# Six of the sixteen products of ones at the head become 22 rounds of eight small products

## The chip, the core and the metric

The kernel runs on one core of a Trainium2 chip. The metric is the device time of one execution in microseconds (us), the median of several runs. The core has five engines with queues of their own: TensorE (PE, with its weight loads listed apart as PEld), VectorE (DVE), ScalarE (ACT), GpSimd (POOL) and SyncE (SP), which here only issues DMAs.

## What is computed

One decoder layer in float32 on x of shape (2, 1024, 256), that is 2048 tokens in 16 tiles of 128:

```python
x = x + attn(layernorm(x), w_qkv, w_out, alpha, beta)   # two decaying prefix scans per channel
x = x + xattn(layernorm(x), ctx, ctx, fside, mask, ...) # 16 heads of 64, 154 keys
x = x + ffn(layernorm(x), ...)                          # 8 experts, top 2, and one shared expert
```

The first step projects the normed tokens to q, k, v; q and k go through elu(.)+1; k and k*v are scanned along time with a decay per head (`out[t] = d*out[t-1] + x[t]`), once with alpha and once with beta; the scans are multiplied by q, divided by their sums over a head and multiplied by w_out. The change touches none of this: the products of ones write a part of PSUM that nothing reads before it is overwritten.

## The kernel before

All work is written out by hand, one instruction list per engine, with semaphores between them. PSUM is one tensor `pb` of eight banks of 512 float32 per partition; a small helper, `Banks`, hands the banks out in turn from bank 0. `w.wait_ge(sem, n)` makes an engine wait.

The tokens of the first step go in four chunks of 512 (`c` = 0 to 3). For a chunk, VectorE takes means and variances of x (L1086, L1088), GpSimd makes the reciprocal roots (L1660 to L1665), ScalarE and VectorE write the normed rows `xn` (L841, L1098), TensorE transposes them (`turned`, L394), ScalarE copies the result to `xnT` (L831), and TensorE projects it (`project`, L440). ScalarE turns k and q into phi (L870, L871), VectorE multiplies (L1118, L1125) and scans (L1140). `densum` (L458) sums over a head with a matrix of 128 rows by 32 columns, `divided` (L469) spreads the result back with tiles of 32 rows.

TensorE's list starts with the function that the change edits, and then the first products that need data:

```python
idle_products()   # 16 products of ones, all to bank 7
keys(0, 2)        # L409: waits for ctxT and the first half of Wk
turned(1, 0)      # L394: waits for xn of chunk 0
project(0, "k", 0, 2)
scan_rest(0)
```

`idle_products` waits only for the fill of `ones` by GpSimd (L1714), so it runs while the first inputs are on their way. `keys(0, 2)` writes banks 0 and 1, `turned(1, 0)` banks 2 and 3, and the projections begin with bank 4. No semaphore ties the products of ones to what follows: TensorE's own order does.

Every float32 product stands in the trace as two records of PE and two of PEld; a transpose stands as one of each.

Later, in cross attention, `product` (L565 and L569) holds the only place where products on tiles of 32 rows and 64 columns are issued. In each call eight products of 128 rows by 64 columns are followed by eight of 32 rows by 64 columns, each of these on another tile of the array, with 256 columns streamed.

Of the kernel before, what the change touches and what calls it, by code (L numbers as in the profile page):

```python
# [171 lines left out]
def decoder(nc, A, xs, out):  # L172
    with ExitStack() as ctx:
        def sb(name, shape, dt=F32):
            return ctx.enter_context(nc.sbuf_tensor(name, shape, dt))
# [7 lines left out]
        pb = ctx.enter_context(nc.psum_tensor("pb", [P, 8, 512], F32))  # L183
# [6 lines left out]
        ones = sb("ones", [P, P])  # L190
# [190 lines left out]
        def _(e):  # L381
# [271 lines left out]

            def idle_products():
                w.wait_ge(zeroed.sem, zeroed["ones"])
                for _ in range(16):
                    e.matmul(pb[:, 7, 0:P], ones[:, :], ones[:, :], start=True, stop=True)

            idle_products()
            keys(0, 2)  # L660
            turned(1, 0)
# [1345 lines left out]
```

## Time and profile before

| what | value |
|---|---|
| median of three runs | 582.8 us (581.6 to 583.47) |
| the profiled execution's own time | 583.38 us |
| its span, first to last instruction | 581.5 us |
| around the span | 1.88 us |
| PE busy | 562.7 us (97%) |
| DVE busy | 441.7 us (76%) |
| ACT busy | 326.0 us (56%) |

A share of busy time is a mean over stages with different limits, and a matmul record has a modelled end that includes the latency of the pipeline: records that start 0.11 us apart can each be shown as 0.27 us long. The pace of a stream on PE is therefore read from starts: the length of a merged row, less the length of one record, over the number of records less one.

### The profile page before, as it was taken

Reading aid. Unit: us, or ns where it says so; the run is one execution under the profiler, and the core shown is the slowest. Engines: PE = TensorE matmul, PEld = TensorE weight load, DVE = VectorE, ACT = ScalarE, POOL = GpSimd, SP = SyncE. Lnnn points to the kernel's source line nnn. Section 1 sums busy time; section 2 is a strip of 40 time slices with the busy share of each in tenths; the row PEclk is TensorE's granted clock in tenths of the full one; section 3 lists DMA queues with packets and bytes.
Section 4 is the critical chain, followed back from the end, with each engine's and each line's share of the span. In section 5 each row is a group of like instructions: output and inputs, shape, how many; then the busy total and the mean of one; then the engine's idle time right before and its main releaser. Section 6 shows DMA issues by size and latency. Waiting matters only on the chain.

```text
span 581.5 us, 11126 instructions
## 1 busy us (share of the span) xinstructions
PE 562.7 (97%) x3656; PEld 426.0 (73%) x3656; DVE 441.7 (76%) x838; ACT 326.0 (56%) x1005; POOL 232.7 (40%) x228
## 2 busy tenths in 40 slices
PE   8999999999999999999999999999999999999992
PEld 6547566788697978888788787878777776676661
DVE  3999999999886879958788679866677556566651
ACT  3632424368869796795976939715232245555220
POOL 1010110307590834477334581626235433444434
PEclk9999999999999999999999999999999999999997
DMA  8920004162741231522316107892654443343424
GB/s 302 349 100 2 1 1 174 45 217 91 275 152 68 93 127 34 185 74 90 130 37 218 55 23 231 261 393 94 172 129 83 64 67 62 54 67 48 60 31 45
DMA packets 36183, 68.37 MB, mean 118 GB/s; under 512 B 5504, under 2 KB 29024, under 8 KB 33632
## 3 DMA queue, kind: packets, MB, share of 16 engines
q1 hardware_dynamic: 28208, 57.99, 29.9%
q0 software_dynamic: 6784, 8.95, 9.3%
q10 hardware_dynamic: 1136, 0.73, 0.4%
q8 instruction: 30, 0.49, 0.4%
q14 instruction: 25, 0.20, 0.1%
HBM read 56.62 MB, written 15.25 MB: 124 GB/s over the span
## 4 chain that ended last, share of the span: by engine, by line
PE 56%; DVE 20%; DMA 9%; issue 8%; POOL 4%; ACT 2%; POOLq 0%; DVEq 0%; SPq 0%
PE pb L744 7%; DMA out_dram<-R 6%; PE pb L636 6%; DVE R L1140 6%; PE pb L499 6%; PE pb L601 6%; PE pb L549 6%; PE pb L565 5%; PE pb L516 4%; PE pb L648 4%; PE pb L778 4%; DVE R L1163 3%; PE pb L613 2%; PE pb L569 2%; DMA out_dram<-R,hidx 2%
## 5 line engine op out<-in xcount | busy, mean ns | idle before, releaser
L896 ACT ACTIVATE R<-R,mx 128x154 f32<-128x154 f32 x256 | 104.4, 415 | 0.1
L1761 POOL DMA_INDIRECT out_dram<-R x36 | 56.1, 1557 | 82.9 <-DMA out_dram<-R 41.7
L744 PE MATMUL pb<-R 128*128 x256 | 81.0, 459 | 0.0
L1022 ACT ACTIVATE R<-R 128x352 f32<-128x352 f32 x36 | 17.9, 497 | 90.4 <-DVE R L1572 74.9
L744 PEld LDWEIGHTS pb<-R 128*128 128x128 f32 x256 | 46.2, 190 | 20.4
L499 PE MATMUL pb<-xnT,wq 128*128 128x256 f32 x256 | 58.2, 383 | 0.0
L887 ACT ACTIVATE R<-pb,bq 128x256 f32<-128x256 f32 x64 | 30.1, 474 | 47.9 <-PE pb L499 47.8
L499 PEld LDWEIGHTS pb<-xnT,wq 128*128 128x128 f32 x256 | 47.7, 190 | 7.8 <-issue 1.2
L908 ACT COPY R<-pb 128x512 f32<-128x512 f32 x80 | 40.8, 614 | 18.4 <-PE pb L549 18.3
L1685 POOL DMA_INDIRECT xs_dram<-xn,pos x32 | 31.7, 991 | 47.3 <-DVE pos L1324 39.0
L896 ACT ACTIVATION_READ_ACCUMULATOR R<-R,mx 128x1 f32 x256 | 49.5, 193 | 0.0
L1660 POOL TENSOR_TENSOR sd<-mv,cst 128x4 f32<-128x4 f32 x12 | 9.8, 815 | 97.9 <-DVE mv L1088 97.8
L1219 DVE SCALAR_TENSOR_TENSOR R<-R 128x2464 f32<-128x2464 uint8 (+1 forms) x18 | 48.7, 2711 | 0.0
L778 PE MATMUL pb<-R 128*128 (+1 forms) x192 | 47.1, 381 | 1.5 <-ACT R L1031 1.5
L1208 DVE TENSOR_TENSOR R<-pb,R 128x924 f32<-128x924 f32 (+1 forms) x48 | 45.2, 996 | 2.7 <-PE pb L516 2.7
L1226 DVE TENSOR_REDUCE mx<-R 128x16 f32<-128x2464 f32 (+1 forms) x18 | 43.7, 2428 | 0.3
L636 PE MATMUL pb<-xnT,sw 128*128 128x256 f32 (+1 forms) x192 | 43.4, 381 | 0.0
L440 PE MATMUL pb<-xnT,R 128*128 128x512 f32 x96 | 43.0, 599 | 0.3 <-ACT xnT L831 0.3
L601 PE MATMUL pb<-wo,R 128*128 128x256 f32 x192 | 42.5, 380 | 0.0
L601 PEld LDWEIGHTS pb<-wo,R 128*128 128x128 f32 x192 | 36.4, 190 | 5.4 <-issue 0.4
L636 PEld LDWEIGHTS pb<-xnT,sw 128*128 128x128 f32 (+1 forms) x192 | 34.2, 181 | 7.1 <-issue 0.8
L778 PEld LDWEIGHTS pb<-R 128*128 128x128 f32 (+1 forms) x192 | 34.0, 191 | 5.7 <-issue 2.4
(202 smaller groups left out, 1179.1 us busy)
## 6 DMA issues: line engine op xcount, KB each, us to landing
R<-in_fside_dram SPq DMA_DIRECT2D x16, 1232.0 KB, 5.6
R<-in_L_ffn_w_dram SPq DMA_DIRECT2D x16, 352.0 KB
R<-in_mask_dram SPq DMA_DIRECT2D x16, 308.0 KB, 2.9
R<-xs_dram SPq DMA_DIRECT2D x32, 129.0 KB, 2.1
KV<-in_ebias_dram SPq DMA_DIRECT2D x2, 1440.0 KB
out_dram<-x SPq DMA_DIRECT2D x4, 512.0 KB
R<-in_L_ffn_w_dram SPq DMA_DIRECT2D x8, 256.0 KB, 4.3
x<-in_x_dram SPq DMA_DIRECT2D x3, 512.0 KB, 10.9
```

Of the source, the lines that this page charges most:

```text
L440: ins = e.matmul(pb[:, u.i, :], wqkv[:, k, col * P:(col + 1) * P], xnT[:, r, k, :], start=(k == 0), stop=(k == 1))
L499: ins = e.matmul(pb[:, u.i, 0:256], wq[:, k, j * P:(j + 1) * P], xnT[:, r, k, cols], start=(k == 0), stop=(k == 1))
L601: ins = e.matmul(pb[:, u.i, 0:D], oT[:, j, q * P:(q + 1) * P], wo[:, j, :], start=(j == 0), stop=(j == 7))
L636: ins = e.matmul(pb[0:mw, u.i, q * 256:q * 256 + 256], wm[:, k, lo:lo + mw], xnT[:, r, k, cols], start=(k == 0), stop=(k == 1))
L744: ins = e.matmul(pb[:, u.i, 0:F], xsT[:, s % 2, k, :], ew13[:, bass.ds(w_reg[s] * 1408 + q * 704 + k * F, F)], start=(k == 0), stop=(k == 1))
L778: ins = e.matmul(pb[:, u.i, 0:D], sT[0:mw, s % 2, m, :], ew2[0:mw, bass.ds(w_reg[s] * 768 + m * D, D)], start=(m == 0), stop=(m == 2))
L896: ins = e.activation(att[t % 3][:, h, :], att[t % 3][:, h, :], ACT.Exp, bias=mx[:, a4, 1, h:h + 1], accum_out=mx[:, a4, 2, h:h + 1])
L908: e.copy(pT[:, hf, 2 * k:2 * k + 2, :], pb[:, u.i, :].rearrange("p (i q) -> p i q", i=2)).then_inc(free[u.i], 1)
L1208: e.tensor_tensor(att[t % 3][:, 2 * lo:2 * hi, :].rearrange("p (r h) k -> p r h k", r=2), pb[:, u.i:u.i + 2, 0:n * SK].rearrange("p r (h k ...
L1219: e.scalar_tensor_tensor(out=att[t % 3][:, lo:hi, :], in0=mk[:, s, lo:hi, :], scalar=-BIG, in1=att[t % 3][:, lo:hi, :], op0=ALU.mult, op1= ...
L1226: e.tensor_reduce(mx[:, a4, 0, lo:hi], att[t % 3][:, lo:hi, :], AX.X, ALU.max).then_inc(*topped.next((t, hs, 0)))
L1761: e.indirect_dma_start(out=out, out_offset=bass.IndirectOffsetOnAxis(ap=to.bitcast(U32), axis=0), in_=rows, in_offset=None, compute_op=ALU ...
```

## The change

`idle_products` alone is edited. Ten of the sixteen products stay. Behind them come six rounds with 128 columns streamed and sixteen rounds with 64. A round is eight products: for each of the four groups of 32 rows, one to the PSUM partitions 0 to 63 and one to 64 to 127. Row group r writes bank 4 + r. That is 176 products in place of six, or 352 PE records and 352 weight loads in place of 12 and 12. Nothing else is changed on any engine.

```diff
             def idle_products():
                 w.wait_ge(zeroed.sem, zeroed["ones"])
-                for _ in range(16):
+                for _ in range(10):
                     e.matmul(pb[:, 7, 0:P], ones[:, :], ones[:, :], start=True, stop=True)
+                for n, count in ((128, 6), (64, 16)):
+                    for _ in range(count):
+                        for r in range(4):
+                            for to in (0, 64):
+                                e.matmul(pb[to:to + 64, 4 + r, 0:n], ones[32 * r:32 * r + 32, 0:64],
+                                         ones[32 * r:32 * r + 32, 0:n], start=True, stop=True)
```

## Rows read from the trace of the kernel before

**Rows 1.** Profile page, part 1 (busy, share, instructions) and part 3 (instruction queue).

```profile
PE 562.7 (97%) x3656; PEld 426.0 (73%) x3656; DVE 441.7 (76%) x838; ACT 326.0 (56%) x1005; POOL 232.7 (40%) x228
...
q8 instruction: 30, 0.49, 0.4%
```

**Rows 2.** Busy time by stage: stretch, length, engines, granted clock, DMA share, GB/s.

```profile
0.00:15.00 15.00, 12.32 (x56) 9.40 (x57) 5.39 (x23) 5.45 (x10) 3.14 (x14) 1.00 0.90 304
15.00:105.00 90.00, 88.27 (x498) 54.75 (x496) 88.58 (x120) 35.73 (x69) 7.06 (x14) 1.00 0.29 99
```

**Rows 3.** Chain of work that ended last, from the start: start, length, engine and line.

```profile
1.25 3.97 DMA x<-in_x_dram
...
7.98 1.01 POOL rs L1663
...
9.80 0.59 ACT xn L841
10.40 0.09 issue
10.49 0.64 PE pb L394 x4
11.15 0.59 ACT xnT L831
...
11.88 1.97 PE pb L440 x4
...
15.79 2.34 DVE R L1140 x2
```

**Rows 4.** Timeline of PE over the first 20 us: start, length, line, count, wait before.

```profile
0.99 5.83 PE L657 MATMUL pb<-ones 128*128 128x128 f32 x32 [0.99 <-POOL cnt L1715]
7.65 2.31 PE L409 MATMUL pb<-R 128*128 128x308 f32 x8 [0.82 <-DMA R<-in_L_xattn_Wk_dram]
10.49 1.06 PE L394 MATMUL pb<-ident,xn 128*128 128x128 f32 x8 [0.53 <-ACT xn L841]
```

**Rows 5.** The same in short windows inside the products of ones.

```profile
3.29 1.06 PE L657 MATMUL pb<-ones 128*128 128x128 f32 x4
...
5.32 0.94 PE L657 MATMUL pb<-ones 128*128 128x128 f32 x7
```

**Rows 6.** Lines L657 and L409 (first 20 us): durations ns min/median/max.

```profile
L657 PE MATMUL pb<-ones x32: 274/421/583, 1.0 to 6.5; 128*128 128x128 f32 x32
...
L409 PE MATMUL pb<-R x8: 422/422/498, 7.6 to 9.5; 128*128 128x308 f32 x8
```

**Rows 7.** Timeline of PE, one call of `product` (L565, L569) and what follows.

```profile
147.94 1.95 PE L565 MATMUL pb<-R,KV 128*64 128x256 f32 x16
149.81 0.69 PE L569 MATMUL pb<-R,KV 32*64 32x256 f32 x16
150.43 0.33 PE L549 MATMUL pb<-ident,KV 128*128 128x128 f32 x1
```

**Rows 8.** L569 in windows of 10 ns: PE and PEld records running in each.

```profile
149.80:149.81 0.01, 0.00 (x0) 0.00 (x0) 1.00 0.00 0
149.81:149.82 0.01, 0.01 (x2) 0.01 (x2) 1.00 0.00 0
...
149.85:149.86 0.01, 0.01 (x8) 0.01 (x8) 1.00 0.00 0
...
150.06:150.07 0.01, 0.01 (x8) 0.00 (x0) 1.00 0.00 0
150.07:150.08 0.01, 0.01 (x9) 0.00 (x0) 1.00 0.00 0
...
150.12:150.13 0.01, 0.01 (x16) 0.00 (x0) 1.00 0.00 0
```

**Rows 9.** Weight loads by columns loaded (32, 64, 128): durations ns min/median/max.

```profile
L458 PEld LDWEIGHTS pb<-R x120: 106/110/110, 29.9 to 106.1; 128*32 128x32 f32 x120
...
L569 PEld LDWEIGHTS pb<-R,KV x256: 127/130/131, 149.8 to 383.0; 32*64 32x64 f32 x128
...
L409 PEld LDWEIGHTS pb<-R x8: 186/189/189, 7.6 to 9.3; 128*128 128x128 f32 x8
```

**Rows 10.** Timeline of PE, the densest stretch of records: four-tile products at 80 to 86 us.

```profile
80.39 1.07 PE L427 MATMUL pb<-R 128*32 128x256 f32 x16
81.28 1.06 PE L458 MATMUL pb<-R 128*32 128x128 f32 x32
82.27 1.98 PE L440 MATMUL pb<-xnT,R 128*128 128x512 f32 x4
84.18 1.17 PE L469 MATMUL pb<-R,hZ 32*128 32x128 f32 x32
```

## The prediction, made before the changed kernel was run

> **What bounds the kernel now.** I read the page first, for the shares: PE 97%, DVE 76% [rows 1]. Those are means, and the change is at the very start, so the busy time by stage comes next: from 15 to 105 us DVE is busy 88.58 of 90 us [rows 2]. PE's 88.27 us there are not the same thing, since its records overlap in their modelled ends. The chain of waits then says what orders the start: the DMA of x lands at 5.2 us, DVE and POOL make the statistics, ACT's second normed tile ends at 10.39, PE transposes at 10.49, ACT copies at 11.15, PE projects at 11.88, and from 15.79 on it is DVE's scans, one behind the other [rows 3]. So whatever moves the transposes at 10.49 later moves the scans, and with them the whole program, by the same amount; what happens on PE before that costs nothing.
>
> PE's timeline shows what happens there. The products of ones run from 0.99; the keys (L409) start at 7.65, after 0.82 us without work, and were released by the landing of Wk; the transposes start at 10.49, after 0.53 us without work, released by ACT [rows 4]. The last key record starts 2.31 - 0.42 = 1.89 us behind the first, at 9.54 [rows 4, 6]. It streams 308 columns; a record of 128 takes 0.11 us at the later pace (below), so about 0.26: PE is free at 9.80, and the slack ahead of the transposes is 10.49 - 9.80 = 0.69 us. The keys may therefore start as late as 7.65 + 0.69 = **8.34 us** at no cost. This is the number that the new head is held against.
>
> **The removed products.** In the short windows four records starting at 3.29 take 1.06 us; less one duration (0.42, the median) over three that is 0.213 us apart. Seven starting at 5.32 take 0.94; less 0.274 over six it is 0.111 us [rows 5, 6]. The second pace is twice the first, that of TensorE's clock at 1.2 and then 2.4 GHz, although the granted clock reads 1.00 all the while [rows 2]: the paces, not that column, tell when it rose. Counted back from the last start at 6.54 (0.99 + 5.83 - 0.28), record 21 is the one at 5.32. Ten products are 20 records, so the part that stays ends at 5.32, nearly all of it at the slow pace, and the part that goes is 12 records, 1.33 us at the fast one.
>
> The Trainium skill ("TensorE: Matmul & The Clock Gate", Part 1) has the clock start low and rise with matmul activity, at a moment that varies from run to run. The two paces agree with it; one trace shows no spread. It changes nothing in the sum.
>
> **The added rounds.** Their only like in the trace is L569: products of 32 rows by 64 columns, eight at a time on eight tiles. It shows all eight at once: from 149.81 to 149.86 eight records start and eight loads with them, about 7 ns apart, and the next eight start between 150.07 and 150.13, once the first have streamed their 256 columns [rows 8]. So a round costs what one tile needs for its two passes, not eight times that.
> - A round with 128 columns: two passes of 0.111 us, 0.22 us. Six: 1.33 us.
> - A round with 64 columns: half the streaming is 0.11 us, and sixteen records at 7 ns are 0.11 us too. The weight load may be a little longer: 130 ns with 64 columns against 189 with 128 is 0.92 ns a column, 59 ns a pass, 0.12 us a round [rows 9]. Sixteen rounds: 1.75 to 1.9 us.
> - The change of tile shape: L565's last record starts at 147.94 + 1.95 - 0.38 = 149.51 and streams 0.21, to 149.72; L569 starts at 149.81, 0.09 later. On the way back 150.13 + 0.21 = 150.34 against L549's 150.43, again 0.09 [rows 7, 8]. Two changes: 0.18 us.
>
> Sum: 5.32 + 0.18 + 1.33 + 1.75 to 1.9 = 8.6 to 8.7 us for the start of the keys. Against 8.34 that is **0.25 to 0.4 us** of delay of the transposes, which the chain passes on whole. ACT's eviction of the first key (behind its normed tiles, which end at 10.39 [rows 3]) still finds its bank filled. The banks 4 to 7 are first used by the projections, behind the rounds on PE's own queue, so no new wait arises. No DMA is added by the program, and no DMA issue stands on PE.
>
> Taken against the profiled execution (583.38 us, of it 581.5 span and 1.88 around it) this makes 583.7. The median of the runs is 0.6 lower, so for it I say 582.8 + 0.3 = **583.1 us**.
>
> **What that rests on, and its bounds.** L569 shows one round of sixteen records; the change issues 352 without a pause. Whether PE's sequencer can hand over a pair of load and matmul every 7 ns for 3 us is shown nowhere. From below nothing helps: the streaming alone gives 3.1 us. From above, the longest dense runs are L458 and L469, 32 records each on four tiles: (1.06 - 0.27)/31 = 25 ns and (1.17 - 0.27)/31 = 29 ns apart [rows 10]. But there four tiles with 0.107 us a pass cannot go faster than 27 ns, so streaming explains them and they set no floor. Over a longer stretch, the 84 records from 80.39 to the last start at 85.08 are 56 ns apart on average, with four projections of 0.43 us a record among them that explain the mean as well [rows 10]. I take L569's pace, because its tile shape is the very one, and keep 29 and 56 ns for the rivals.
>
> **Rivals.**
> 1. *A long stream is bound by the hand-over of instructions, at 25 to 29 ns a record.* 352 records take 8.8 to 10.2 us in place of 3.1; the keys start at 5.5 + 8.8 to 10.2 = 14.3 to 15.7, 6.0 to 7.4 us past 8.34. The time is 589 to 590, slower by 1.1%. It decides from where the rounds take 2 us more than I say, at some 15 ns a record. For it: what I have is a burst of 16, and PE stood waiting ahead of it, so those instructions may all have been queued. Against it: nothing in the trace runs slower than its streaming. The Trainium skill ("TensorE: Matmul & The Clock Gate", "Wait — 56ns, not 53.3ns?") gives a floor of about 25 ns from start to start of matmuls however small, which would be this rival. Here L569's starts 7 ns apart on different tiles contradict it for a burst; for a stream of rounds no row does.
> 2. *It is slower still, up to 56 ns a record, or the instructions do not arrive.* 7312 PE records against 0.49 MB in 30 packets are 67 bytes each and 16 KB a packet [rows 1], so the rounds need nearly three packets more within 3 us, while the DMA engines are full of inputs (share 0.90 over the first 15 us [rows 2]). At 56 ns the rounds take 19.7 us and the time is 582.8 + 25.2 - 8.3 = 599.7; one late packet would cost a few us. Slower by 1 to 3%.
> 3. *The clock is low for the rounds or falls in them* because small tiles count for less, or because it rises later in that run. All at the slow pace: the rounds take 6.2 us, keys from 11.7, eight records of 0.51 us to 15.8, 5.3 past 10.49, and the first four projections 1.7 us more: 582.8 + 7 = 590. A rise one us later costs about half a us.
> 4. *Faster.* The only way is a clock that in some runs falls in PE's gaps (0.82 and 0.53 us) and would not with the first gap filled. The row at 7.65 shows the keys at the fast pace (1.89/7 = 0.27 us for 308 columns), and the fastest run of before is 1.2 us below the median, 0.2%: less than can be told.
>
> **How the numbers follow.** Streaming bound, my forecast, 0.52, with its own range 582.4 to 585 (a late rise of the clock, twice the cost of a round's edge). Rival 1: 0.22. Rival 2: 0.12. Rival 3: 0.09. Rival 4: 0.05. The range must leave out at most 2 in 10: it drops rival 2 above 592 and the tails below 581.8, and so is 581.8 to 592. About 0.3%, 1.75 us, is what a measurement of this kernel can tell from no change. Faster by more: 0.03, from rival 4. Within it: 0.02 of rival 4 and 0.48 of the forecast. Slower by more: 0.04 of the forecast (a late rise) and rivals 1 to 3, 0.47.
>
> **What would show it.** PE's timeline of the changed kernel: L657's tile records should fill 5.4 to about 8.6 us, at 14 ns a record in the wide rounds and 7 in the narrow ones, and the first L409 should start at 8.6 to 8.7. If it starts after 14, rival 1 or 2 is right, and the pace in the narrow rounds tells which: an even 25 to 29 ns is the hand-over, jumps of a microsecond or more are missing instructions. Rounds at 0.43 us with wide columns are the clock. The transposes L394 should start at 10.7 to 10.9, and everything from DVE's first scan on should be shifted by that 0.25 to 0.4 us, with every later stage as long as before. If the stages behind 15 us have other lengths than before, the prediction is wrong in a way that I have no step for.

## The result and the profile after

The changed kernel takes 596.46 us (median of 4 runs, 595.0 to 597.6) against 582.42 for the one before (4 runs): a ratio of 1.0242, 95% interval 1.0208 to 1.0275, 14.0 us more. I had forecast 583.1, and 581.8 to 592 for the range: wrong, on the slow side.

| | before | after |
|---|---|---|
| median | 582.42 us | 596.46 us |
| profiled execution, its own time | 583.38 us | 595.0 us |
| its span | 581.5 us | 593.1 us |
| PE records | 3656 | 3996 |
| first record of the keys (L409) | 7.65 | 19.70 |
| first transpose of chunk 0 (L394) | 10.49 | 23.21 |
| first projection (L440) | 11.88 | 24.58 |

All of it is at the head. This is PE's timeline of the changed kernel over its first 45 us (start, length, line, shape, count, wait before); the rows that answer [rows 4] are the first, the fifth and the sixth. L662 is the line of the rounds.

```profile
0.99 4.57 PE L657 MATMUL pb<-ones 128*128 128x128 f32 x20 [0.99 <-POOL cnt L1721]
5.49 2.76 PE L662 MATMUL pb<-ones 32*64 32x128 f32 x203
12.59 2.25 PE L662 MATMUL pb<-ones 32*64 32x64 f32 x128 [4.35 <-issue]
19.07 0.69 PE L662 MATMUL pb<-ones 32*64 32x64 f32 x21 [4.22 <-issue]
19.70 3.68 PE L409 MATMUL pb<-R 128*128 128x308 f32 x8
23.21 1.03 PE L394 MATMUL pb<-ident,xn 128*128 128x128 f32 x8
24.58 10.54 PE L440 MATMUL pb<-xnT,R 128*128 128x512 f32 x24 [0.33 <-ACT xnT L837]
```

The 352 tile records do not come in one stream. After 203 of them PE stands still for 4.35 us, then does exactly 128, stands still for 4.22, and does the last 21. Both pauses are put down to "issue": PE waited for no semaphore. The other two things to see are the keys, 3.68 us in place of 2.31, and the instruction queue of the page's part 3, which had 30 packets and 0.49 MB before [rows 1]:

```profile
q8 instruction: 33, 0.54, 0.4%
```

The clock, in stretches of the same trace (stretch, length, PE busy and records, granted clock, share of the DMA engines, GB/s):

```profile
0.00:12.00 12.00, 7.25 (x223) 1.00 0.84 288
12.00:15.00 3.00, 2.25 (x128) 0.53 1.10 361
15.00:19.00 4.00, 0.00 (x0) 0.50 1.06 386
19.00:23.00 4.00, 3.93 (x29) 0.57 1.04 384
```

It goes to half, 1.2 GHz, at 12.2 us, near the end of the first pause, and stays there until 22.4. That is why the keys run slow.

Further on the two traces match. L440 starts 12.70 us later than before, the last chunk's transposes at 407.92 against 395.25, 12.67 later, and the last PE record ends 12.7 later. Only the tail behind PE, the last scattered writes, is 1.1 us shorter in this execution, which makes the 11.6 us by which the two profiled times differ. The medians differ by 14.0, 1.3 more than the 12.7 of the head. The profiled execution of before is near the upper end of what its four runs took, that of the changed kernel is the lowest of its four, and the runs of each spread over 1.9 and 2.6 us; the traces can't assign the 1.3.

### The profile page after: what moved, and what is told of

It reads as the page before. It is cut to its first block, busy times and chain, and to the rows that moved or that the text cites. A ratio compares the mean times of both kernels' runs of the same rounds, so it can differ in the third digit from the quotient of the medians.

```text
span 593.1 us, 11806 instructions
## 1 busy us (share of the span) xinstructions
PE 568.2 (96%) x3996; PEld 430.9 (73%) x3996; DVE 441.9 (75%) x838; ACT 325.8 (55%) x1005; POOL 232.8 (39%) x228
## 4 chain that ended last, share of the span: by engine, by line
PE 55%; DVE 20%; issue 9%; DMA 8%; POOL 4%; ACT 2%; POOLq 0%; DVEq 0%
PE pb L750 6%; DMA out_dram<-R 6%; PE pb L636 6%; DVE R L1146 6%; PE pb L499 6%; PE pb L601 6%; PE pb L549 6%; PE pb L565 5%; PE pb L516 4%; PE pb L784 4%; PE pb L648 3%; DVE R L1169 3%; DMA out_dram<-R,hidx 2%; PE pb L569 2%; DVE R L1124 2%
## 5 line engine op out<-in xcount | busy, mean ns | idle before, releaser
L440 PE MATMUL pb<-xnT,R 128*128 128x512 f32 x96 | 43.0, 599 | 0.3 <-ACT xnT L837 0.3
## 6 DMA issues: line engine op xcount, KB each, us to landing
KV<-in_ebias_dram SPq DMA_DIRECT2D x2, 1440.0 KB, 10.5
x<-in_x_dram SPq DMA_DIRECT2D x3, 512.0 KB, 12.2
```

Source lines behind the costliest of these rows:

```text
L440: ins = e.matmul(pb[:, u.i, :], wqkv[:, k, col * P:(col + 1) * P], xnT[:, r, k, :], start=(k == 0), stop=(k == 1))
```

## The experiments

Theory A: each pause is a wait for PE's own instructions. The middle burst of 128 records with their loads is 256 instructions. Three packets more for 340 more pairs of load and matmul fit a packet of that size. They are fetched while the inputs fill the DMA engines. Theory B: the pauses belong to the tiles, their four banks or the hand-over of such instructions. All kernels of this study compute the whole layer. The ratio given with each run is the recorded one, with its 95% interval; it differs by up to 0.13% from the quotient of the two medians beside it.

**Streaming without the instructions.** First the head with nothing for the rounds, then the same streaming in full products.

```diff
-                for n, count in ((128, 6), (64, 16)):
-                    ...
```

> The changed kernel without its 22 rounds: ten products of ones alone. Theory A (the two pauses of 4.3 us inside the rounds are waits for the next 16 KB of PE's instructions, fetched by DMA while the inputs fill the DMA engines): no pause, the keys start at 7.65 as before; the time is that of before within 0.2% unless the clock falls in the 2.3 us without products. Theory B (the pauses come from the tile form, its four banks or the hand-over of its instructions): the same here. Rival on the clock: the clock is low for the keys, they take 4.1 us in place of 2.3 and the time is 1 to 3 us longer.

Measured: 583.91 us (6 runs) against 581.87 for before (27 runs), ratio 1.0046 (1.002 to 1.0071).

```profile
7.53 3.81 PE L409 MATMUL pb<-R 128*128 128x308 f32 x8 [1.90 <-DMA R<-in_L_xattn_Wk_dram]
11.18 1.04 PE L394 MATMUL pb<-ident,xn 128*128 128x128 f32 x8
```

No pause without a cause, the keys at 7.53, but slow: eight records in 3.81 us in place of 2.31, half the pace for most of them. So the clock's rival is right here, and the six products that the change removed were worth 0.7 us of the transposes. The median is 2.0 us longer; 1.3 of it is not seen at the head.

```diff
-                for _ in range(10):
+                for _ in range(24):
```

This replaces the ten products of the run above.

> Ten products and, in place of the rounds, 14 more full products of ones with 128 columns: the streaming of 6 wide and 16 narrow rounds in 28 records in place of 352. Theory A and B: no pause, the keys start at 8.4 to 8.5, the transposes 0.1 to 0.2 us later than before; time 582.4 + 0.1 to 0.3. It prices the streaming of the change without its number of instructions.

Measured: keys at 8.49, transposes at 10.64, 0.15 later than before, as said. The time: 583.76 (9 runs), ratio 1.0038 (1.0025 to 1.005); run again as e10 over 12 runs it was 582.7 against 581.32, ratio 1.0013 (0.9995 to 1.0031).

> 24 full products again, with more rounds. Its head delays the transposes by 0.1 to 0.2 us; if that is all, the ratio is within 1.001. If the earlier 0.3 to 0.4% repeats, it is real and its place is the landing of the second chunk of x (12.7 us against 12.0) and what DVE's order puts behind it.

The head of the second profile was not as expected: the 48 records of ones took 7.99 us in place of 7.34, the keys came at 8.82 and the transposes at 10.90, 0.41 later than before. The columns that the rounds stream, in 28 records, cost about 2 us in the first measurement, and in the second nothing that can be told from zero.

**How many instructions bring the pause.**

```diff
-                for n, count in ((128, 6), (64, 16)):
+                for n, count in ((128, 6), (64, 6)):
```

> 6 wide and 6 narrow rounds, 192 tile records. In the changed kernel PE ran dry behind record 223 (20 full and 203 tile records). Theory A: the rounds run through and end near 8.0, the keys start there (records 213 to 220), and PE runs dry in the keys or the transposes, near record 223, until the next packet lands at about 12.5; transposes about 2 us late, time +1.5 to +2.8 us. Theory B: no pause behind the last tile record; time within 0.5 us of before.

```profile
0.99 4.62 PE L657 MATMUL pb<-ones 128*128 128x128 f32 x20 [0.99 <-POOL cnt L1721]
5.55 2.67 PE L662 MATMUL pb<-ones 32*64 32x128 f32 x192
8.58 2.31 PE L409 MATMUL pb<-R 128*128 128x308 f32 x8 [0.36 <-DMA R<-in_L_xattn_Wk_dram]
10.73 0.38 PE L394 MATMUL pb<-ident,xn 128*128 128x128 f32 x2
12.75 0.82 PE L394 MATMUL pb<-ident,xn 128*128 128x128 f32 x6 [1.63 <-issue]
13.89 10.54 PE L440 MATMUL pb<-xnT,R 128*128 128x512 f32 x24 [0.33 <-ACT xnT L837]
```

This is PE's timeline of that kernel, and it decides between the theories. All tile records run through. The pause comes between the second and the third transpose of the next stage, where no tile and no bank of the rounds is involved: behind record 20 + 192 + 8 + 2 = 222, against 20 + 203 = 223 in the changed kernel. It ends at 12.75, against 12.59 there. The projections start 2.0 us later than before; the median is 586.22 (10 runs), ratio 1.0068 (1.0048 to 1.0089), some 4 us, of which the head shows these 2.0.

```diff
-                for n, count in ((128, 6), (64, 16)):
+                for n, count in ((128, 6),):
```

> Six wide rounds alone, 96 tile records, over by about 7.0. Theory A: record 223 is now reached at about 25 us, long after its packet; no pause, keys at 7.65, time as before within 0.2%. Theory B (tile form or banks): a pause could come at any number of records; time + up to a few us.

Measured: no pause, the tile records over by 7.2, keys at 7.41, transposes at 10.34, none of it later than before. The time was 583.79 (10 runs), ratio 1.003 (1.0013 to 1.0046), and run again as e11, over 12 runs, 582.99 against 581.32, ratio 1.0023 (1.0007 to 1.0039).

> Six wide rounds again, with more rounds. The head delays nothing; if that is all, the ratio is within 1.001. If the earlier 0.3% repeats, it is real, and its place is the landing of the second chunk of x (13.2 us against 12.0) and what DVE's order puts behind it.

So 96 tile records cost no pause, but some 1 to 2 us remain that PE's head does not explain. The traces show two places. First, in both profiles the second chunk of x landed late: DVE took it up at 13.21 and 13.34 us, against 12.01 before, and its statistics stand ahead of the first scan in DVE's list. That scan starts at 16.69 and 16.82, against 15.79 before: 0.90 and 1.03 later, though the transposes were earlier. With 24 full products DVE took the chunk up at 12.71 in one profile and 11.85 in the other, so the landing varies between executions. Second, in e4_rounds6 and e2_full24 the granted clock falls to half once more, near 32 us, behind a gap of PE. In the same stretch of before it stays at 1.00. These are rows of e4_rounds6 (the first with the granted clock, 0.60, in front of DMA share and GB/s) and, last, one of before:

```profile
32.00:36.00 4.00, 4.00 (x22) 1.79 (x15) 3.83 (x11) 0.30 (x1) 1.93 (x4) 0.60 0.41 172
32.34 3.33 PE L440 MATMUL pb<-xnT,R 128*128 128x512 f32 x4
38.24 2.48 DVE L1188 TENSOR_TENSOR R<-pb,R 128x512 f32<-128x512 f32 x4 [1.03 <-PE pb L469]
31.43 1.98 PE L440 MATMUL pb<-xnT,R 128*128 128x512 f32 x4
```

Four projection records take 3.33 us in place of 1.98, and DVE, the busy engine there, waits 1.03 us for PE in both of these profiles; before and the second profiles of the two kernels (e10, e11) have no such wait. In e4_rounds6 the two places make 1.9 us by the fifth scan (41.36 against 39.46), as much as the medians differ. How often each occurs in the executions without a profile is not known. As a control:

```diff
-                for _ in range(16):
+                for _ in range(15):
```

> Fifteen products of ones in place of sixteen, nothing else. The head's sum gives no change: the keys wait for Wk until 7.65 anyway. If the time is within 0.15% of before, the 0.3% that the runs with 24 products and with six rounds lost beyond the shift of their transposes comes from what they run at the head; if it is 0.3% slower too, it goes with any edit of the head.

Measured: 581.79 (10 runs), ratio 1.0007 (0.9988 to 1.0027). This edit of the head costs nothing. Whether the rounds push the landing of x, or make the second fall of the clock more frequent, is left open; by the two ratios of six rounds it is 0.2 to 0.3%.

**The form of the products, with the same number of instructions.** Against the changed kernel:

```diff
-                for n, count in ((128, 6), (64, 16)):
-                    ...
+                for _ in range(176):
+                    e.matmul(pb[0:32, 7, 0:32], ones[:, 0:32], ones[:, 0:32], start=True, stop=True)
```

> The same number of instructions as the changed kernel, but 176 products of 128 rows by 32 columns with 32 columns streamed, all on one tile and in one bank, inputs as in the changed kernel. Theory A: PE runs dry behind record 223 and again 128 records later whatever their form; the records go 25 to 30 ns apart, so the packets are asked for 1 to 3 us later and the pauses end near 14 and 20 us; keys from about 20.5. Theory B (tile form or banks at fault): no pause, 352 records end at 14 to 16 us.

```profile
5.56 6.68 PE L659 MATMUL pb<-ones 128*32 128x32 f32 x203
13.63 4.21 PE L659 MATMUL pb<-ones 128*32 128x32 f32 x128 [1.40 <-issue]
20.11 0.82 PE L659 MATMUL pb<-ones 128*32 128x32 f32 x21 [2.27 <-issue]
20.86 2.34 PE L409 MATMUL pb<-R 128*128 128x308 f32 x8
```

One tile, one bank, and the very same pattern: 203, 128, 21. The records go 32 ns apart, so more of the fetch is covered and the pauses are shorter, but the bursts start 6.48 us apart (13.63 and 20.11), exactly as in the changed kernel (12.59 and 19.07). Theory B is out; the interval is a packet's. 594.01 us in one run. The clock stayed up here (keys in 2.34 us), with pauses of 1.40 and 2.27 in place of 4.35 and 4.22.

**The same instructions where the DMA engines are idle.** The kernel before, with the 176 small products ahead of `contents(0)`:

```diff
                     u = bank.take(("con", b, n))
                     w.wait_ge(free[u.e], u.empty)
+                    if b == 0 and n == 0:
+                        for _ in range(176):
+                            e.matmul(pb[0:32, u.i, 0:32], ones[:, 0:32], ones[:, 0:32], start=True, stop=True)
```

> The kernel before, with the 176 small products of the run on one tile set ahead of the first product of contents(0), at about 51 us, where the DMA engines are idle. Theory A: records run 25 to 30 ns apart over three packets without a pause over 1 us; the time grows by up to 10 us because they stand on PE's queue. Theory B': if PE's own fetch or hand-over is slow whatever the DMA load, pauses of several us appear here too.

PE's timeline, and then the windows of 0.01 us in which the trace has DMA bytes (the last two numbers are the DMA share and GB/s):

```profile
53.30 11.33 PE L421 MATMUL pb<-ones 128*32 128x32 f32 x352
```

```profile
57.79:57.80 0.01, 0.01 (x6) 1.00 5.91 1638
61.57:61.58 0.01, 0.01 (x6) 1.00 6.42 1638
65.25:65.26 0.01, 0.01 (x2) 1.00 6.76 1638
```

352 records in one run without a pause, (11.33 - 0.20)/351 = 32 ns apart. With nothing else on the DMA engines the packets can be seen: 1638 GB/s for 0.01 us are 16 KB, all booked at one moment, and they come 3.78 and 3.68 us apart. PE needs 4.06 us for 128 records here, so the supply just keeps up. 593.82 us in one run.

**The changed kernel with its inputs held back.** SP's list waits, behind the first DMAs of x, until the last product of the rounds has raised the new semaphore `headed`:

```diff
+            w.wait_ge(headed, 1)
             e.dma_start(wk[:, :, 0:512], wkv[:, :, 0:512]).then_inc(in_wk[0], 16)
```

> The changed kernel with SP's list held behind the first DMAs of x: the first half of Wk and all that follows are issued only when the last round has run, so that the DMA engines are nearly idle from about 5.5 us on. Theory A (each pause is a wait for a 16 KB packet of instructions behind the inputs): the packets now land within some 2 us, both pauses shrink to under 1 us or vanish, and the rounds end at 9 to 10 us in place of 19.7. Theory B (tile form, banks, hand-over): two pauses of 4.3 us as before, rounds to 19 us. The total time says nothing here, since the inputs come later.

```profile
5.56 3.54 PE L663 MATMUL pb<-ones 32*64 32x128 f32 x203
10.62 1.58 PE L663 MATMUL pb<-ones 32*64 32x64 f32 x128 [1.52 <-issue]
14.36 0.69 PE L663 MATMUL pb<-ones 32*64 32x64 f32 x21 [2.16 <-issue]
```

```profile
8.26:8.27 0.01, 0.01 (x26) 1.00 6.93 1638
8.50:11.50 3.00, 1.48 (x138) 1.00 0.00 0
11.74:11.75 0.01, 0.01 (x24) 1.00 8.82 1638
11.75:14.30 2.55, 0.45 (x43) 0.95 0.00 0
```

The pauses shrink from 4.35 and 4.22 us to 1.52 and 2.16, but do not vanish as I had said. The bursts start 3.74 us apart in place of 6.48. A share of 6.93 of 16 engines in 0.01 us is 1.1 us of one engine's time for a packet, yet PE goes on only 2.4 and 2.6 us behind the moment at which it is booked (10.62 and 14.36), and the next one is booked 1.1 us after PE has gone on. So a packet costs 3.7 us with free DMA engines, as between the packets of e7_later, and the inputs add 2.7. The whole took 596.84 us in one run, which says nothing on the pauses, since the inputs come later.

**More of the same.**

```diff
-                for n, count in ((128, 6), (64, 16)):
+                for n, count in ((128, 6), (64, 32)):
```

> 6 wide and 32 narrow rounds, 608 tile records, 256 more than the changed kernel: two packets of instructions more. Theory A (one packet of 256 instructions at a time, 6.5 us each from 12.59 to 19.07 while the inputs load): PE restarts near 12.6, 19.1, 25.5 and 32.0, after 128 records each time; keys at about 32.6, the time 13 us above the changed kernel's. If packets could be fetched side by side, the later pauses would shrink.

```profile
13.10 2.21 PE L662 MATMUL pb<-ones 32*64 32x64 f32 x128 [4.42 <-issue]
19.86 2.25 PE L662 MATMUL pb<-ones 32*64 32x64 f32 x128 [4.54 <-issue]
26.34 2.25 PE L662 MATMUL pb<-ones 32*64 32x64 f32 x128 [4.23 <-issue]
30.34 0.69 PE L662 MATMUL pb<-ones 32*64 32x64 f32 x21 [1.76 <-issue]
```

Bursts of 128 again, 6.76, 6.48 and then 4.00 us apart. The page has 35 packets, two more than the changed kernel's 33 for 512 more instructions. The last interval is short, and from 25 to 31 us the DMA share is 0.80 where it was 1.05 before; 4.00 is near the 3.74 of the idle engines. The kernel took 605.45 us (one run), 10.5 above the changed kernel's profiled execution and 9.0 above its median, not 13: the last burst starts 30.34 - 19.07 = 11.27 us later, of which the two packets are 6.48 and 4.00. The pauses do not shrink as fetches side by side would make them: the packets come one at a time, at the cost of the load at that moment.

## Why the prediction was wrong, by its own steps

**What bounds the kernel, and the slack: right.** The keys could start as late as 8.34 at no cost (with 24 full products they start at 8.49 and the transposes are 0.15 late), and whatever passed that went through whole: L440 is 12.70 us late, the first scan too, the last chunk's transposes 12.67. A second path to the first scan, the landing of the second chunk of x, was missed; with PE as late as here it costs nothing.

**The ten and the six products: right for the time, with a gap.** The rounds started at 5.49, forecast 5.41. But I took the six products as time only. Without them or the rounds PE stands still for 1.90 us before its pace has doubled, and most of the keys run at half pace (e1_ten); with them the keys are fast.

**The price of a round: the mechanism right, a term mis-sized.** Eight tiles do run at once. e4_rounds6 has 96 wide records in 1.65 us, (1.65 - 0.27)/95 = 14.5 ns, forecast 14. e3_rounds12 has 96 narrow ones in 1.02 us more, and its last record is 0.05 shorter: 11 ns, where L569's burst had given 7 [rows 8]. A narrow round is 0.18 us, not 0.11 to 0.12. With unbroken supply the rounds would by this estimate have taken 1.4 + 2.8 = 4.2 us in place of 3.1 to 3.2, and cost 1 us more. The sentence that four tiles cannot go faster than 27 ns stands beside its own row of 25; nothing hangs on it.

**The step that failed** is "I take L569's pace, because its tile shape is the very one": a burst of 16 records priced a stream of 352. What bounds the stream is none of the shape's properties but the supply of instructions: 128 records per 6.48 us, 51 ns each, while the inputs load, and 3.74 us, 29 ns each, when nothing does. Behind a start of 223 records this is all PE gets. I had written 29 and 56 ns as the outer ends of the unknown cost, but from rows that do not show this mechanism.

**Rival 2 was the right one,** with 0.12. It had the packets at 16 KB, nearly three too many, and engines full of inputs. What it lacked was a price: "one late packet would cost a few us" should have been worked out. By the page of before, w_qkv took 7.5 us from issue to landing in that stretch; two packets one behind the other at that, less the 3 us that the rounds last, are 12 us, outside my range. That is an estimate made afterwards, and it comes near the measured 12.7 partly by luck: a packet took 6.5 us. Its other half, 56 ns for every record, was not the way it went: the pace is fast within a burst. **Rival 1,** an even 25 to 29 ns, is refuted for tiles, by the bursts. **Rival 3,** the clock, came as a consequence of the pauses: from the first on the granted clock is 0.50, the second burst goes (2.25 - 0.31)/127 = 15.3 ns apart, and the keys take 1.37 us more. Its late rise occurs too, in other kernels: the same first 203 tile records took 2.76 us here, but 3.12 in e9_rounds38 and 3.54 in e5_held, where the first of them last 416 ns in place of 267. The pause behind them hides it. **Rival 4** did not occur as a gain; that the clock falls behind PE's gaps in some executions and not in others is what e4_rounds6 and e2_full24 show near 32 us.

Where the 12.7 us are, in the two traces: from 5.49 to the keys at 19.70 it is 2.76 us of rounds, 4.35 of pause, 2.25, 4.22 of pause and 0.69, less 0.06 where rows overlap: 14.21. Before, the keys came 2.33 us behind record 21 (5.32 to 7.65), and the rounds start 0.17 later than that record did: 14.21 + 0.17 - 2.33 = 12.05 for the keys' start. Slow keys add 1.37, and the 0.53 us that PE had waited ahead of the transposes are gone, with 0.17 of overlap: 12.72 at the transposes.

The section "Instruction fetch mechanics" of the Trainium skill's page "Runtime: NRT & Kernel Launch" has the sequencer refill its instructions in blocks of 16 KiB, 256 instructions, and calls crossing a block mostly hidden. The runs agree with the size: 128 records with their loads in each burst. They disagree with "hidden": a pause of 1.4 to 4.5 us at every block that was used up in under 3.7 us, or under 6.5 with the inputs loading.

What stays open: 1.3 us of the 14.0 between the medians, what brings the late landing of x and the second fall of the clock, where the profiles of six rounds lose their time, and why a packet takes PE 3.7 us when its transfer takes 1.1 us of one DMA engine.

No variant beat the kernel before; fifteen products equal it.

## What to carry to other kernels

Count instructions as well as cycles wherever many small ones stand together, above all at the head, where the inputs load: a stream is only as fast as its instructions arrive, here one packet of 256 each 3.7 us, or 6.5 us under the inputs, once the stock at the start is used up. A burst that fits in what is already there says nothing of a stream. To fill PE's waiting time take the largest products that do it: 28 records streamed as many columns as the 352 and made the transposes 0.15 and 0.41 us late, against 12.7.

## What the runs showed of the hardware that was not expected

- PE's instructions come in packets of 256 (128 records and their loads): bursts of 128 in four kernels, and two packets more for 512 instructions more. 222 or 223 records could run at the start, 446 instructions, which would be two packets if the waits and whatever else stands ahead of them make up the rest (an estimate; the trace doesn't list these). The rest comes one packet at a time: 3.68 to 3.78 us with idle DMA engines, 6.48 to 6.76 with a DMA share above 1.
- The granted clock in the first microseconds reads 1.00 where the pace is half: 0.213 us a record of 128 columns [rows 5], and in e1_ten the keys at 3.81 us in place of 2.31 under a clock of 1.00.
- A pause of 4.35 us took the granted clock to 0.50. Pauses of 1.40 and 2.27 with a burst of 4.21 between them did not (e6_onetile); pauses of 1.52 and 2.16 with a burst of 1.58 between them did, at 14.1 us, near the end of the second (e5_held).
- The fall is not the same in all executions: behind a gap of 2.38 us and one of 0.40 it came in e4_rounds6 (1.03 us of wait for DVE), behind 2.45 and 0.40 in e11_rounds6b, the same kernel, it did not.
- Products of 32 rows by 64 columns, eight at once, start 11 ns apart in a stream with 64 columns, and 128 x 32 products on one tile 32 ns apart.
